# Message pass of a graph network: a fourth pipeline stage for the sum, and gathered rows handed back at the first product

## The reference, cut to what matters

```python
x = jnp.concatenate([h[src], h[dst], edge_attr], axis=-1)   # 128 + 128 + 64 values an edge
x = jax.nn.gelu(x @ mW1 + mb1)
x = jax.nn.gelu(x @ mW2 + mb2)
msgs = x @ mW3 + mb3
agg = jax.ops.segment_sum(msgs, dst, num_segments=h.shape[0])
```

## Time and profile before

| | us |
|---|---|
| median of 3 runs | 9064.03 (9042.72 to 9085.63) |
| the profiled execution | 9004.81, span of its trace 9003.1 |
| first to last instruction of the message pass, about | 3447 to 4979, some 1,532 |

### The profile page before, as it was taken

How to read it: one execution, slowest core, us unless ns; L and a number is a source line. 1 busy time by engine, 2 the same in 40 slices (tenths; PEclk the granted TensorE clock), 3 DMA queues, 4 the chain that set the end, 5 groups by cost and what they waited for, 6 DMA issues and landing times. The chain is left out here.

```text
span 9003.1 us, 154403 instructions
## 1 busy us (share of the span) xinstructions
PE 5685.8 (63%) x44934; PEld 4616.3 (51%) x44935; DVE 5133.5 (57%) x12349; ACT 2748.7 (31%) x6113; POOL 3659.2 (41%) x3623
## 2 busy tenths in 40 slices
PE   1111117666677775888888357777773777777666
PEld 1000003655577673555555246666662666666566
DVE  7444444999668673333333456666665666666612
ACT  1000000588557552344333212222221222222210
POOL 2666661234000004555555245555551555555300
PEclk9999999888899897898888677888885888888788
DMA  4111113234324223344446023333352333333555
GB/s 159 44 43 43 46 41 139 86 128 140 111 101 156 98 101 85 112 119 118 116 114 105 15 82 93 95 94 98 96 95 47 93 96 95 94 97 96 64 185 191
DMA packets 662769, 884.50 MB, mean 98 GB/s; under 512 B 304425, under 2 KB 487254, under 8 KB 643668
## 3 DMA queue, kind: packets, MB, share of 16 engines
q1 hardware_dynamic: 553028, 674.48, 23.4%
q0 software_dynamic: 109568, 207.74, 11.6%
HBM read 648.77 MB, written 233.08 MB: 98 GB/s over the span
## 5 line engine op out<-in xcount | busy, mean ns | idle before, releaser
L989 POOL DMA_INDIRECT rows<-head_table,idxb x1760 | 1707.7, 970 | 1614.6 <-issue 484.7
L989 POOL DMA_INDIRECT rows<-source_table,idxb x880 | 844.3, 959 | 1800.8 <-ACT idxb L1009 1157.4
L1702 DVE TENSOR_REDUCE gtop<-ps_top 128x1 f32<-128x512 f32 x1760 | 1208.6, 687 | 382.9 <-remote 207.1
L363 POOL DMA_INDIRECT records<-recb,idxb x784 | 768.2, 980 | 440.4 <-issue 372.0
L1839 PE MATMUL ps_top<-srow,sel 128*128 128x128 bf16 x7040 | 668.4, 251 | 297.6 <-DVE gtop L1702 240.2
L1839 PEld LDWEIGHTS ps_top<-srow,sel 128*128 128x128 bf16 x7040 | 549.4, 115 | 401.2 <-DVE gtop L1702 306.5
L391 PE MATMUL ps_g<-hott 64*128 64x128 bf16 x784 | 59.7, 302 | 989.1 <-DVE prior L456 593.8
L1851 PE MATMUL ps_acc<-val,hot 128*128 128x132 f32 x3520 | 615.4, 324 | 95.1 <-issue 72.4
L787 PE MATMUL ps_cells<-hot 128*128 128x128 bf16 x4608 | 481.3, 248 | 255.1 <-DVE hot L745 122.2
L1096 PE MATMUL ps_acc<-rows,pt 128*128 128x128 f32 x3750 | 517.6, 280 | 135.2 <-DVE pt L1117 120.8
L1851 PEld LDWEIGHTS ps_acc<-val,hot 128*128 128x128 f32 x3520 | 532.6, 226 | 131.7 <-issue 101.2
(11 more groups left out here) (327 smaller groups left out, 12548.1 us busy)
## 6 DMA issues: line engine op xcount, KB each, us to landing
logs<-log_counts SPq DMA_DIRECT2D x75, 1600.0 KB
hot<-one_hots SPq DMA_DIRECT2D x440, 256.0 KB
wt<-edge_weights SPq DMA_DIRECT2D x50, 1600.0 KB
one_hots<-hot SPq DMA_DIRECT2D x220, 256.0 KB
hott<-one_hots_t SPq DMA_DIRECT2D x440, 128.0 KB
edge_weights<-both SPq DMA_DIRECT2D x125, 320.0 KB, 2.8
log_counts<-none SPq DMA_DIRECT2D x125, 320.0 KB, 2.2
records<-blank SPq DMA_DIRECT2D x16, 1870.0 KB
```

Of the source, the lines that this page charges most:

```text
L363: g.indirect_dma_start(out=recs[:, :], out_offset=bass.IndirectOffsetOnAxis(ap=idxb[k][:, t:t + 1], axis=0), in_=recb[k][:, t, :], in_offs ...
L989: g.indirect_dma_start(out=rows[r][:, k, :], out_offset=None, in_=table, in_offset=bass.IndirectOffsetOnAxis(ap=idxb[r][:, k:k + 1], axis= ...
L1702: ve.tensor_reduce(gtop[:, h:h + 1], ps_top[h % TOPS][:, :], AX.X, ALU.max).then_inc(topped, 1)
```

## The change

The pass gets four stages in place of three. The stage "last" is split: the second product, its bias, its gelu and the index copy belong to the new stage "second"; the sum over the edges and the addition to the accumulator stay in "last", one group behind. The sum now stands first in PE's step and the addition first in DVE's. POOL's gather into a buffer waits for `sum1` of the group that used it (the last reading of the rows), no longer for `agg_done`. `blocks` loads 11 values a turn.

```diff
@@ gather_rows: the parameter agg_done is now called used
-        wait(g, agg_done, n - RING + 1)
+        wait(g, used, n - RING + 1)
@@ mlp_pass, POOL
-                    gather_rows(g, table, rows, idxb, idx_ready, rows_in, agg_done, begun)
+                    gather_rows(g, table, rows, idxb, idx_ready, rows_in, sum1, begun)
@@ mlp_pass, PE
-                        last, mid, first = stages
+                        last, second, mid, first = stages
                         if last:
                             i, r, _ = last
+                            g, k = RING * i + r, r % 2
+                            pe.wait_ge(gelu2, g + 1)
+                            pe.wait_ge(wcol, g + 1)
+                            wait(pe, acc_done, g - 1)
+                            for q in range(TG):
+                                ins = pe.matmul(ps_acc[k][:, 0:MA], hot[r][:, q, :], g2[k][:, q, :],
+                                                start=q == 0, stop=q == TG - 1)
+                            ins.then_inc(agg_done, 1)
+                        if second:
+                            i, r, _ = second
                             g, k = RING * i + r, r % 2
                             pe.wait_ge(gelu1, g + 1)
 ...
-                        if last:
...
-                    pipeline(nc, pe, c, 3, step)
+                    pipeline(nc, pe, c, 4, step)
@@ mlp_pass, DVE
-                        last, _, first = stages
+                        last, second, _, first = stages
                         if last:
                             i, r, b = last
+                            g, k = RING * i + r, r % 2
+                            ve.wait_ge(agg_done, g + 1)
+                            wait(ve, acc_done, g)
+                            ve.tensor_tensor(c.acc[:, bass.ds(b, 1), 0:MA], c.acc[:, bass.ds(b, 1), 0:MA],
+                                             ps_acc[k][:, 0:MA].unsqueeze(1), ALU.add).then_inc(acc_done, 1)
+                        if second:
+                            i, r, _ = second
                             g, k = RING * i + r, r % 2
 ...
-                        if last:
...
-                    pipeline(nc, ve, c, 3, step)
+                    pipeline(nc, ve, c, 4, step)
@@ mlp_pass, ACT
-                        last, mid, first = stages
-                        if last:
-                            i, r, _ = last
+                        _, second, mid, first = stages
+                        if second:
+                            i, r, _ = second
 ...
-                    pipeline(nc, act, None, 3, step)
+                    pipeline(nc, act, None, 4, step)
```

More of the change, by code:

```diff
@@ L978, in _, with gather_rows @@
                         sp.wait_ge(stored, 16)
-def gather_rows(g, table, rows, idxb, idx_ready, rows_in, agg_done, begun):
+def gather_rows(g, table, rows, idxb, idx_ready, rows_in, used, begun):
     def gather(i, r):
```

## The result

The changed kernel took 9176.99 us (median of 4 runs, 9157.58 to 9210.25) against 9053.38 us (4 runs, 9036.72 to 9085.63): a ratio of 1.0136, with a 95% interval of 1.0092 to 1.018. It is slower by 124 us. Its profiled execution took 9210.25 us, with a span of 9208.5 us.

A forecast was written before the change was run, and what follows sets the result against it. It took PE as busy 5.62 of 6.96 us a group, its signals late while POOL's gathers run. Terms -10 + 127 + 5 = +122 us on the 9064 us median gave 9186 us; 8-in-10 range 9000 to 9330 us.

The forecast's parts named there:

- The order is one list: In the pass, PE, DVE and ACT keep the same order of work; only the loop's seam moves: 0 us.
- The seam, -10 us: Block-number loads of PE and DVE at 27 loop seams move: 16 us gained less 6 paid for the eleventh value.
- The release is the index copy: POOL's next gathers are released by the index copy behind the second gelu, no longer by the sum; no size alone.
- Case A, 7.90 us: POOL's gathers, one batch at a time: batch, late signal, bias to index copy and restart take 7.90 us, against 6.45.
- Case B, 15.37 us for two: Two of POOL's gather batches run on end before the next release: 15.37 us for two groups, 7.69 a group.
- 1.2 us on half of the groups, 127 us: In the pass, 106 groups each lose 1.2 us through PE signals held at the moment of release: +127 us.
- The start, +5 us: At the start of the pass nine gather batches run on end, so PE stands still one batch longer: +5 us.
- Where the waits would show: In the pass, bias and second gelu wait longer than 241.4 and 634.3 us; PE idles longer ahead of the sum.
- Other passes unchanged: Only the message pass grows, from 1532 to some 1650 us; all other passes stay unchanged.
- The earlier release pays: Rival: groups close up towards PE's 5.62 us, half of 263.9 us idle time goes: 8932 us; chance 0.18.
- All pay 1.2 us: Rival: batches on end starve PE throughout the pass, all 212 releases cost 1.2 us: 9313 us; chance 0.14.
- No effect: Rival: same order in the pass, and hold-ups come from something the batches only accompany: 9054 us; chance 0.26.

The follow-up runs named there:

- rotation alone: The changed kernel with gathers again waiting for `agg_done`: 9040.28 us against 9037.9, ratio 1.0011; on another chip 7762.94 us against 7769.42, ratio 0.9993.
- release alone: The kernel before with gathers waiting for `sum1` instead of `agg_done`, three stages kept: 9135.11 us against 9037.9, ratio 1.0115; on another chip 7774.25 us, ratio 1.0006.
- four ahead: Gathers held to at most four groups ahead instead of eight: changed kernel 8980.7 us, ratio 0.9947; kernel before, on another chip, 7754.76 and 7761.3 us.
- plain DMAs: The kernel before with this pass's indirect gathers replaced by as many plain DMAs of fixed table rows from POOL's queue: 8598.31 us against 9037.9.

## Why the prediction came out right

It said 9186 us, slower, for the release's sake. Measured are 9177 us. Point by point:

- **The order is one list.** Right. Counts by line are those of before but for the missing records, mean durations differ with the clock (L1417 751 ns, before 699), and the rotation alone costs 1.0011 and 0.9993, both with 1 in their intervals.
- **The seam, -10 us.** The term was wrong, though small. On DVE the 77.5 us ahead of the weight column are gone as foreseen. On prompt chips, where it can be read cleanly, what stands ahead of the weight column with the old order (72.0 us in 23 cases, release alone) stands ahead of the addition with the new one (63.4 us in 32, rotation alone). In both every eighth interval between second products is longer, 6.75 and 6.59 us against some 4.9 (from the ninth to the 209th). A seam costs 1.7 to 1.8 us wherever it stands. I had taken the addition's own wait to cover the load; the rate shows that it does not, and whether a load, and of which engine, or the turn of the loop makes it was not tried.
- **The release is the index copy.** Right: the earlier trace rows named the sum 90 times, the profile of after the index copy 109 times.
- **Case A, 7.90 us.** Measured 7.90 us on the mean after (38 cases, neither on end), and 7.62 with the release alone. The sum was 4.69 + 1.12 + 1.45 + 0.64, where 4.69 is the measured batch; 4 x 0.94 + 3 x 0.30, as it was written, is 4.66. With the release at the first product's signal and four ahead the 1.45 fall away, which leaves 6.45 us, and 6.66 are measured.
- **Case B, 15.37 us for two.** Measured 14.96 us (86 cases). But the text ascribed part of the price to batches on end. In the traces pairs were there before as well, at 13.32 us, no dearer than two singles.
- **1.2 us on half of the groups, 127 us.** The product was right and neither factor was. Nearly all batches are paced by the index copy (38 singles, 86 pairs), but a group costs not 1.2 us more but 0.69 (7.47 less 6.78). The present group was modelled at 6.45 us and takes 6.78, and against that a group of a pair costs 0.70 us more (14.96 / 2) where a single one costs 1.12. 0.69 x 220 = 152 us is what the profiled execution shows; the medians moved by 124, with the release alone by 97. I had the count of hold-ups of the earlier trace rows for the share of groups that pay, and that was a guess that two errors made good.
- **The start, +5 us.** Right. Nine batches run on end where eight did, with and without the rotation, and from the first second product to the third it is 48.4 and 48.6 us with the new release, 45.5 and 42.2 with the old.
- **Where the waits would show.** Half wrong. The second gelu waits longer, 687.7 us against 634.3. The bias waits less, 154.5 against 241.4, and PE less ahead of the sum and second product. The transposes' signal is now later as well (1.87 us against 1.31), so that DVE stands ahead of the copy and PE ahead of the first product, and waits that stood behind are shorter for it. I had followed only the signal that the release passes through, and not asked what each of PE's signals meets in the moved batch: that of the first product is even less late (0.73 us against 1.63). The granted clock fell to 0.85 and the pass grew by 150 us, as foreseen in kind.
- **Other passes unchanged.** In work they are; in this profiled execution they were some 50 us longer, and on the late chip of the experiments the same.

**The rivals.** "The earlier release pays" fell: the release alone costs 1.15% on the late chip and gives nothing on a prompt one (1.0006). "All pay 1.2 us" fell with the factor above. "No effect" is what happens on a prompt chip. On the late chip it is refuted as a mechanism: the second product's signal is late by 2.58 us with the release alone and by 0.03 with plain DMAs. The Trainium skill, page "SBUF — State Buffer", section "Who interferes with whom", says "PE and ACT never wait on anyone". It speaks there of ports to SBUF. The prompt traces agree with it (0.03 us of lateness under the gathers); the late ones show late signals of PE and not what PE waits on, so what failed is the step from that rule to hold-ups that do not stem from the gathers.

**What stays open.** Why one kind of chip holds PE's signals during gathers, and the other does not, or whether it is the chip at all. Whether form, scattered rows or length of the batch does it. What is held, the end of PE's matmuls, which the profile only models, or the passing of its signals: the timeline shows matmuls starting during a batch (4131.53 above), so PE does run, and the signals of DVE and ACT pass in time. The first comparison alone would have had me write a rule of the kernel; the same change costs 1.4% in one place and nothing in another.

## What to carry to other kernels

Before a release is moved earlier, ask what becomes the release then: here it was the index copy at the end of a chain of product, bias, gelu and copy, whose last three take 1.45 us that the sum's own signal does without. An engine that is never waited for (POOL: 2 us) can still set the pace through what its work does to the others, so give it no more groups of lead than it needs. Four were better than eight by 15 us on a prompt chip (at the end of the pass, as far as its traces show) and, with the early release, by 57 us against the kernel before on a late one; three were too few. And measure such a change on more than one chip before you keep or drop it.

## What the runs showed of the hardware

The same kernel takes 9038 us on one chip and 7769 us on another, with the same gathers, the same dense stage and repeats within 1% on each. The whole difference lies in stages in which POOL gathers indirectly (of 1249 us between the profiled executions of before on a late chip and the rotation alone on a prompt one 192 before the dense stage, 350 in this pass, 707 in the two attention passes behind it). On the late kind the second product's signal reaches DVE 1.4 us late on the mean, while DVE's signal reaches ACT in 0.03 us and ACT's reaches PE in 0.2 us or less in nearly every wait, and eight batches on end can stop all other engines for over 10 us; with plain DMAs in the same places that is gone and the pass takes 1100 us instead of 1518. The granted clock of 0.88 goes with the idle time: with that gone it was 0.99 of 2.4 GHz.
